# Rows of a 4-expert layer go back to their tokens by scatters inside the block loop instead of by gathers behind it

## What is computed

```python
x = x + 0.5 * _L0_ffn_ref(_layernorm(x), W1, b1, W2, b2, Wg, bg)   # 4 experts, one per token
x = x + _L0_attn_ref(_layernorm(x), ...)                          # "attention 0", no score matrix
x = x + 0.5 * _L0_ffn_ref(_layernorm(x), ...)                     # 4 experts again
x = x + 0.5 * _L1_ffn_ref(_layernorm(x), expert_sel, keys, values)  # 32 experts, top 4
x = x + _L1_attn_ref(_layernorm(x), ...)                          # softmax attention, 16 heads
x = x + 0.5 * _L1_ffn_ref(_layernorm(x), ...)                     # 32 experts again

# _L0_ffn_ref: the expert with the highest gate logit, alone, counts for a token
idx = argmax(softmax(x @ Wg + bg))
y[e] = gelu(x @ W1[e] + b1[e]) @ W2[e] + b2[e]
out = y[idx]
```

## Time and profile before

| | us |
|---|---|
| three runs | 2506.00, 2508.28, 2508.82; median 2508.28 |
| the profiled execution | 2506.18 |
| its span in the trace | 2504.4 |

### The profile page before, as it was taken

The page is one execution under the profiler, slowest core; times in us unless marked ns, Lnnn a source line. Parts: engine busy times, 40 slices in busy tenths (PEclk is TensorE's granted clock), DMA queues, the critical chain, the costliest instruction groups (busy, mean ns, idle before and its releaser), DMA issues.

```text
span 2504.4 us, 36012 instructions
## 1 busy us (share of the span) xinstructions
PE 2246.4 (90%) x11234; PEld 1562.8 (62%) x11234; DVE 1981.3 (79%) x4636; ACT 1297.6 (52%) x1907; POOL 991.8 (40%) x849
## 2 busy tenths in 40 slices
PE   4489488849869999996999999999999999999999
PEld 3367366637647777774555555555555555778777
DVE  5578487748759999976888888888888886888887
ACT  1088332338724444442666666666666665444444
POOL 5600688620056777752222111121111213565654
PEclk9999665569979999997999999999999999999999
DMA  7144221134268888861122211112111115888897
GB/s 177 61 161 139 38 32 37 30 113 153 93 139 177 182 178 177 184 140 54 57 68 69 63 59 60 59 56 61 59 56 60 57 55 108 175 178 183 176 185 153
DMA packets 148497, 266.81 MB, mean 107 GB/s; under 512 B 19347, under 2 KB 30614, under 8 KB 148118
## 3 DMA queue, kind: packets, MB, share of 16 engines
q1 hardware_dynamic: 132790, 247.99, 41.0%
q0 software_dynamic: 15584, 17.25, 3.3%
HBM read 213.26 MB, written 54.31 MB: 107 GB/s over the span
## 4 chain that ended last, share of the span: by engine, by line
PE 41%; DVE 5%; DMA 5%; issue 3%; ACT 1%; POOL 0%; SPq 0%; DVEq 0%; POOLq 0%; ACTq 0%
PE ps L2010 12%; PE ps L2034 10%; PE ps L2021 9%; DMA gate_rows<-gates_dram 4%; DVE m L1408 2%; PE ps L1729 2%; PE ps L1731 2%; PE ps L1730 2%; PE ps L2043 1%; PE ps L2076 1%; DMA gates_dram<-gateT 1%; DVE shift L1575 1%; DVE lo L1070 1%; PE ps L1743 1%; PE ps L2068 1%
## 5 line engine op out<-in xcount | busy, mean ns | idle before, releaser
L1575 DVE TENSOR_REDUCE shift<-ps 128x1 fp32r<-128x512 f32 x1024 | 663.6, 684 | 146.5 <-PE ps L2010 141.7
L993 ACT ACTIVATE prob<-ps 128x1024 f32<-128x1024 f32 x512 | 509.9, 1024 | 352.8 <-PE ps L2021 345.1
L842 ACT ACTIVATE hi<-m 128x512 fp32r<-128x512 f32 x512 | 318.9, 631 | 414.2 <-DVE m L1408 414.1
L692 POOL TENSOR_TENSOR lo<-m,hi 128x512 fp32r<-128x512 f32 x256 | 342.3, 1339 | 305.8 <-ACT hi L842 305.2
L2010 PE MATMUL ps<-k_pad,q_st 128*128 128x512 f32 x1024 | 401.0, 433 | 13.2 <-DVE shift L1575 7.0
L1408 DVE SCALAR_TENSOR_TENSOR m<-ps,gate_rows 128x512 f32<-128x512 f32 x512 | 334.4, 679 | 84.1 <-PE ps L1731 51.2
L2010 PEld LDWEIGHTS ps<-k_pad,q_st 128*128 128x128 f32 x1024 | 179.2, 190 | 256.0 <-DVE shift L1575 175.6
L2021 PE MATMUL ps<-q_sh,k_pad 128*128 128x512 f32 x1024 | 330.3, 404 | 0.0
L2034 PE MATMUL ps<-prob,v_cols 128*32 128x512 f32 x2048 | 272.8, 605 | 0.4 <-ACT prob L993 0.4
L1070 DVE TENSOR_TENSOR lo<-m,hi 128x512 fp32r<-128x512 f32 x256 | 210.5, 822 | 16.9
L1729 PE MATMUL ps<-hi,vals_hl 128*128 128x512 f32 x512 | 209.6, 409 | 0.7 <-DVE lo L1070 0.4
(11 more groups left out here) (218 smaller groups left out, 3996.5 us busy)
## 6 DMA issues: line engine op xcount, KB each, us to landing
gate_rows<-gates_dram SPq DMA_DIRECT2D x256, 512.0 KB, 6.3
w_blk<-w_dram SPq DMA_DIRECT2D x38, 514.5 KB, 3.6
q_st<-q_dram SPq DMA_DIRECT2D x64, 256.0 KB, 2.6
k_pad<-k_dram SPq DMA_DIRECT2D x256, 50.0 KB
k_dram<-qk_hl SPq DMA_DIRECT2D x48, 256.0 KB
q_dram<-qk_hl SPq DMA_DIRECT2D x48, 256.0 KB
x_blk<-sorted_x SPq DMA_DIRECT2D x38, 256.0 KB, 3.4
sorted_y<-yb_rows SPq DMA_DIRECT2D x38, 256.0 KB, 2.0
```

What stands on the lines that cost most here:

```text
L692: pool.tensor_tensor(m["lo"][:, s], m["m32"][:, s], m["hi"][:, s].bitcast(F32), ALU.subtract).then_inc(sig(ph, "lo_pool"), 1)
L842: return act.activation(o, i, ACT.Copy)
L993: act.activation(prob[:, h % HP, 2 * half:2 * half + 2, :], ps[:, b0:b0 + 2, :], ACT.Exp, scale=SCALE).then_inc(sig(ph, "prob"), 1)
L1575: dve.tensor_reduce(shift[:, g % 2, b, c:c + 1], wide(PASS1 + b % 2), AXX, ALU.max, negate=True).then_inc(sig(ph, "qmax"), 1)
```

## The change

- Each row of `sorted_x` is 129 floats wide (`DX`): the 129th is the number of its token. `apply_norm` copies it beside the normalised row, from a constant `token` that SP loads at the start. The filler rows behind an expert's last row carry the number `NOWHERE` = 16384, beyond every token; so do 512 rows at the end of `sorted_x`, where blocks without work now read (one more fill on SP in ph 0).
- SP's `save`, `plan_back`, `y_row`, `y_idx` and all gathers of output rows go. Instead Pool runs `scatter_y(ph)` during the layer, ahead of its barrier: per block one copy of the token numbers to int32 (`y_goes_to`, two blocks ahead) and four indirect DMAs that scatter `yb_rows` to the tokens' rows of `y_dram`; indices above 8191 are left out (`bounds_check`). `y_rows` of block n waits until these of block n-2 have landed.
- After ph 0 `collect(t)` is one plain accumulating DMA per tile on Pool, from 512 consecutive rows of `y_dram`. In ph 3 SP loads the rows plainly (`rows_back`): tiles 0 to 2 behind the barrier, every other tile behind the `gates` of the tile two before it; VectorE waits for `rows_here`.
- The plan of the blocks has one step more.

The core of the diff:

```diff
+DX = D + 1
+NOWHERE = 2 * TOKENS
...
+    c["token"] = (SEQ * np.arange(TILES)[None, :, None] + BLK * np.arange(P)[:, None, None]
+                  + np.arange(BLK)[None, None, :]).astype(np.float32).reshape(P, -1)
...
+            sp.dma_start(token[:], const["token"]).then_inc(early_in, 16)
...
-                    sp.dma_start(free, zeros[:]).then_inc(filled, 16)
+                    sp.dma_start(free, nobody[:]).then_inc(filled, 16)
+                if ph == 0:
+                    sp.dma_start(sorted_x[ROWS0:ROWS0 + SEQ, :].rearrange("(p s) d -> p s d", s=BLK),
+                                 nobody[:]).then_inc(filled, 16)
...
+                    if i >= WB:
+                        sp.wait_ge(sig(ph, "y_to"), n0 + i - WB + 1)
...
-                def save(i):
-                    n, q = n0 + i, (n0 + i) % 2
-                    sp.wait_ge(sig(ph, "yb_rows"), n + 1)
-                    sp.dma_start(sorted_y[i * SEQ:i * SEQ + SEQ, :].rearrange("(p s) d -> p s d", s=BLK),
-                                 yb_rows[q][:]).then_inc(y_there[q], 16)
...
-                        sp.wait_ge(filled, 16 * E0 * (turn + 1))
+                        sp.wait_ge(filled, 16 * (E0 * (turn + 1) + 1))
                     load_x(i)
-                for i in range(NB0):
-                    if i + WB < NB0:
-                        load_w(i + WB)
-                        load_x(i + WB)
-                    save(i)
+                for i in range(NB0 - WB):
+                    load_w(i + WB)
+                    load_x(i + WB)
...
+            def rows_back(n, q):
+
+                if not (isinstance(n, int) and n < 2):
+                    pass_wait(sp, sig(2, "x_done"), n * 4 - 4)
+                sp.dma_start(y_back[q][:], y_dram[bass.ds(n * SEQ, SEQ), :].rearrange("(p s) d -> p s d", s=BLK))\
+                  .then_inc(rows_here[q], 16)
+
+            sp.wait_ge(phase_end, 4 * 3)
+            for q in range(2):
+                sp.wait_ge(y_there[q], 64 * ((2 * NB0 + 1 - q) // 2))
+            for n in range(3):
+                rows_back(n, n % 2)
             gates(0, 0, first=True)
...
-            with sp.Fori(1, PAIRS) as pair:
-                gates(pair * 2, 0)
-                gates(pair * 2 + 1, 1)
+            rows_back(3, 1)
+            with sp.Fori(1, PAIRS - 1) as pair:
+                for q in range(2):
+                    gates(pair * 2 + q, q)
+                    rows_back(pair * 2 + (2 + q), q)
+            gates(TILES - 2, 0)
+            gates(TILES - 1, 1)
...
-                    if ph == 3 and gather and fb in (0, 2, 4, 6):
-                        collect_on(t, 1 - p, fb // 2)
...
-                def collect_on(t, q, b):
-
-                    if b == 0:
-                        pass_wait(pool, sig(ph, "y_idx"), t + 1)
-                    pool.indirect_dma_start(
-                        y_back[q][:, b, :], None, sorted_y,
-                        bass.IndirectOffsetOnAxis(ap=y_idx[:, q, b:b + 1], axis=0)).then_inc(back[q], 16)
...
-                        for n in range(3):
-                            collect(2, n)
...
+            def y_goes_to(ph, i):
+
+                n = FIRST_BLOCK[ph] + i
+                pool.wait_ge(w_here[n % WB], 32 * (n // WB + 1))
+                pool.tensor_copy(y_to[:, n % 4], x_blk[n % WB][:, :, D]).then_inc(sig(ph, "y_to"), 1)
+
+            def scatter_y(ph):
+
+                for i in range(2):
+                    y_goes_to(ph, i)
+                for i in range(NB0):
+                    n = FIRST_BLOCK[ph] + i
+                    pool.wait_ge(sig(ph, "yb_rows"), n + 1)
+                    if i + 2 < NB0:
+                        y_goes_to(ph, i + 2)
+                    pool.wait_ge(sig(ph, "y_to"), n + 1)
+                    for b in range(BLK):
+                        pool.indirect_dma_start(
+                            y_dram, bass.IndirectOffsetOnAxis(ap=y_to[:, n % 4, b:b + 1], axis=0),
+                            yb_rows[n % 2][:, b, :], None, bounds_check=TOKENS - 1,
+                            oob_is_err=False).then_inc(y_there[n % 2], 16)
...
+            def collect(t):
 
                 if t == 0:
-                    pool.wait_ge(sig(ph, "y_row"), ph // 2 + 1)
                     for q in range(2):
-                        done = ph // 2 * NB0 + NB0
-                        pool.wait_ge(y_there[q], 16 * ((done + 1 - q) // 2))
-                if t >= 2 and ph == 0:
-                    pool.wait_ge(sig(1, "stats"), t - 1)
-                elif t >= 2:
-                    pool.wait_ge(sig(ph, "x_done"), 4 * (t - 1))
-                for b in range(BLK):
-                    c = t * BLK + b
-                    rows = bass.IndirectOffsetOnAxis(ap=y_row[:, c:c + 1], axis=0)
-                    if ph == 0:
-                        pool.indirect_dma_start(x[:, c, :], None, sorted_y, rows,
-                                                compute_op=ALU.add).then_inc(back[t % 2], 16)
-                    else:
-                        pool.indirect_dma_start(y_back[t % 2][:, b, :], None, sorted_y,
-                                                rows).then_inc(back[t % 2], 16)
+                        pool.wait_ge(y_there[q], 64 * ((NB0 + 1 - q) // 2))
+                else:
+                    if t >= 2:
+                        pool.wait_ge(sig(1, "stats"), t - 1)
+                pool.dma_start(x[:, t * BLK:t * BLK + BLK, :],
+                               y_dram[t * SEQ:t * SEQ + SEQ, :].rearrange("(p s) d -> p s d", s=BLK),
+                               accum_op=ALU.add).then_inc(back[t % 2], 16)
...
                 scatter(0, t)
+            scatter_y(0)
             barrier(pool, 1)
...
             barrier(pool, 2)
+            scatter_y(2)
             barrier(pool, 3)
...
+                    dve.tensor_copy(dst[:, :, D], token[:, t * BLK:t * BLK + BLK])
...
-                dve.wait_ge(back[t % 2], 64 * (ph // 2 * (TILES // 2) + t // 2 + 1))
+                dve.wait_ge(rows_here[t % 2], 16 * (t // 2 + 1))
...
+                    pc.step(dve.tensor_scalar(begin_f[:], row_f[:], last_row[:, 0:1], float(2 * ROWS0), ALU.is_gt,
...
-                        dve.wait_ge(y_there[n % 2], 16 * (n // 2))
+                        dve.wait_ge(y_there[n % 2], 64 * (n // 2))
...
-                    if i == 1:
-                        plan_back()
...
-                    if ph == 3 and two_on and fb == 13:
-                        dve.tensor_copy(y_idx[:, p], y_row[:, bass.ds((t + 4) * BLK, BLK)])\
-                           .then_inc(sig(ph, "y_idx"), 1)
...
-                        dve.wait_ge(back[p], (t - p) * 32 + 64 * (TILES // 2 + 2))
+                        dve.wait_ge(rows_here[p], (t - p) * 8 + 32)
```

More of the change, by code:

```diff
@@ L47 @@
 NB0 = TILES + E0 - 1
+FIRST_BLOCK = {0: 0, 2: NB0}
 ROWS0 = REGION * E0
+DX = D + 1
+NOWHERE = 2 * TOKENS
 WCOL = 2 * FF0
@@ L209, in macaron @@
         with ExitStack() as first_own:
-            xnr_a = [first_own.enter_context(nc.sbuf_tensor(f"xnr_a{b}", [P, BLK, D], F32)) for b in range(XR)]
+            xnr_a = [first_own.enter_context(nc.sbuf_tensor(f"xnr_a{b}", [P, BLK, DX], F32)) for b in range(XR)]
             stage = [first_own.enter_context(nc.sbuf_tensor(f"stage{b}", [P, 2048], F32)) for b in range(2)]
@@ L225, in macaron @@
         w_hl = [ffn0_sb(f"w_hl{b}", [P, 2, WCOL], F32R) for b in range(2)]
-        x_blk = [ffn0_sb(f"x_blk{b}", [P, BLK, D]) for b in range(WB)]
+        x_blk = [ffn0_sb(f"x_blk{b}", [P, BLK, DX]) for b in range(WB)]
         xb_hl = xnT_hl
         ffn0_own.close()
-        sorted_x = nc.dram_tensor("sorted_x", (ROWS0, D), F32).ap()
-        sorted_y = nc.dram_tensor("sorted_y", (NB0 * SEQ, D), F32).ap()
+        sorted_x = nc.dram_tensor("sorted_x", (ROWS0 + SEQ, DX), F32).ap()
+        y_dram = nc.dram_tensor("y_dram", (TOKENS, D), F32).ap()
         w_dram = nc.dram_tensor("w_dram", (E0, P, WROW), F32).ap()
@@ L251, in macaron @@
         outT = att0_sb("outT", [P, SEQ])
-        xnr_b = [att0_sb(f"xnr_b{b}", [P, BLK, D]) for b in range(XR)]
+        xnr_b = [att0_sb(f"xnr_b{b}", [P, BLK, DX]) for b in range(XR)]
         xnr = {0: xnr_a, 2: xnr_b}
@@ L315, in macaron @@
         back = [sem(f"back{b}") for b in range(2)]
+        rows_here = [sem(f"rows_here{b}") for b in range(2)]
         w_here = [sem(f"w_here{b}") for b in range(WB)]
@@ L616, in _ @@
             pool.memset(neg_half[:], -0.5)
-            pool.memset(zeros[:], 0.0).then_inc(setup, 1)
+            pool.memset(nobody[:, :, 0:D], 0.0)
+            pool.memset(nobody[:, :, D:DX], float(NOWHERE)).then_inc(setup, 1)
             def rstd_of(ph):
@@ L686, in apply_norm, with step @@
                                        ALU.mult).then_inc(sig(ph, "xn"), 1)
-                def step(t, fb, two_on, p=0, gather=False):
+                def step(t, fb, two_on):
                     if fb in POOL_FB:
@@ L811, in _ @@
                     over_tiles(pool, ph, *low_parts(ph, ffn1_mem)[0:2])
```

(21 more changed lines are left out.)

37 lines of the change are left out of this document (15 added, 22 removed).

## The result

The changed kernel takes 2495.73 us (median of 6 runs, 2493.38 to 2499.78), the one before 2507.32 us (6 runs, 2503.92 to 2508.82): a ratio of 0.9953, 95% interval 0.9942 to 0.9963, so 11.6 us less, where 4.1 less were forecast. The profiled executions, one of each kernel, have spans of 2504.4 and 2491.5 us.

The account below looks back on a forecast made before the run. Pool was taken to bound attention 0, TensorE the 4-expert loop and 32-expert layer. Terms -12.8, +1.0, 0.0, +3.8, +2.9, +1.0 sum to -4.1 us: 2504.2 us from median 2508.28; range 2499 to 2509, whole 2494 to 2534.

Parts of the forecast that it names:

- Attention 0, -12.8: Attention 0: one plain accumulating load replaces four gathers on Pool, VectorE's waits go, token copy adds 1.4; -12.8 us.
- The third rival: Attention 0 and first boundary: the plain accumulating load costs Pool what four gathers did, 7.4 us; 2533 us; chance 0.09.
- The block loop, +1.0: 4-expert block loops: scatters bring Pool to 7.0 us a block, casts may wait a little; +1.0 us for both loops.
- The second rival: 4-expert block loop: Pool becomes the bound; 2531 us if a bounds check costs 0.2 us; chance 0.22.
- Both ends of the loop, 0 and +3.8: Boundaries behind the 4-expert layers: barriers left later, shorter loads pay back; 0.0 at the first, +3.8 us at the second.
- The drain: Barriers behind the 4-expert layers: a Pool drain behind indirect DMAs costs 5.0 us, as read behind attention 0.
- part 5: 32-expert layer: 60 gathers leave Pool and 15 index copies leave VectorE, booked at 0; late rows +1.0 us.
- the first rival: Ends of 4-expert loops: drain only waits for landing, or Pool needs 5.5 us a block; 2495 us; chance 0.18.
- Routing, +2.9: Routing of layer 0: fifth fill +1.4, token load +0.5, 16 small copies +1.0; together +2.9 us.
- The 32-expert layer, +1.0: 32-expert layer: y rows queued behind the gates delay each tile some 0.2 us; 13 tiles, +1.0 us in all.
- The fourth rival: 32-expert layer: rows land 2 us late in every tile, +0.9 us a tile; 2515 us; chance 0.06.

Follow-up runs that it names:

- number 8: Changed kernel with one fill of 128x1024 on Pool in each block of both 4-expert layers: 2505.0 us beside 2507.43 for the kernel before.
- number 9: Changed kernel with two fills of 128x1024 on Pool in each block of both 4-expert layers: 2520.71 us, ratio 1.0072 to the kernel before.
- number 3: Changed kernel; Pool waits for its scatters' semaphores instead of draining at the barriers behind both 4-expert layers and attention 0: 2486.25 us, ratio 0.9912.
- number 2: Kernel before, with one more Pool drain in an idle gap in the last tile of the first 32-expert layer: 2503.81 us beside 2508.38.
- number 10: Kernel before with only the wide rows: 129 floats, token copies, token load, fifth fill; ratio 1.0003.
- number 1: Changed kernel with one extra 64 KB Pool DMA at the start of the first 32-expert layer: ratio 0.9960 to the kernel before.
- number 4: Changed kernel; in the first 32-expert layer SP loads y rows ahead of the gates instead of behind them: 2493.19 us.
- number 11: The changed kernel run again, no edit: ratio 0.9948 to the kernel before.
- number 5: Changed kernel; three barriers without drain, y rows ahead of gates, remaining drain in a gap before attention 1: 2471.16 us beside 2502.78.
- number 6: Changed kernel with extra plain 2 KB Pool DMAs, 14 in the first 32-expert layer and four a tile in attention 1: 2490.93 us beside 2502.78.
- number 7: Changed kernel with extra indirect Pool gathers, 15 in the first 32-expert layer and 56 in attention 1: 2509.47 us beside 2502.78.

## Why the prediction was right or wrong

**Attention 0, -12.8: right, by parts that were each off by about 1 us.** Between `xn` of tile 0 and barrier 2 the changed kernel takes 224.9 us for 236.05: 11.2 less, with 1.6 us of a longer drain in it, which is -12.8. In parts: the ramp gave 2.0 for 2.8 (`xn` of tile 5 at 339.23 for 342.29, so from -1.0 to -3.1); from there to the last `xnr_b` (495.81 for 510.46) it is 11.6, where 11.4 of waits less 1.4 of copies were booked, that is 10.0; Pool's scatters behind it end 0.8 us later. The period is 12.12 us for the 12.07 of the earlier trace rows, so the token copy costs some 0.05 and not 0.1. The load takes 0.96 us of Pool for the 1.9 taken, which doesn't matter where Pool waits. The third rival (7.4 us a load) falls.

**The block loop, +1.0: right in sum, by two errors.** Pool was reckoned at 7.0 us a block and needs 5.9. The disturbance was the mis-sized term: 0.4 us a block instead of 1.6 (all 152 scatters have a mean of 1062 ns and a median of 979), the copy 0.19 us for 0.4. I had let every subtraction of VectorE stop a starting DMA. The loop costs nothing (108.9 us between the second and the next to last `yb_rows` in both kernels); the stretch from the first cast to the second `yb_rows`, in which `plan_back` stood, is 0.4 and 0.6 us shorter, which I had put at nothing; the last rows wait 1.0 us longer at each layer, which I had not seen. The second rival was near: numbers 8 and 9 put its point one fill of 0.95 us a block above the changed kernel, and show that it starts softly, over VectorE's casts. A bounds check of 0.2 us, +0.8 us a block, would have come close to it; but scatters with it take 0.97 us for the 0.95 without, so it costs next to nothing.

**Both ends of the loop, 0 and +3.8: off by -1.4 and -1.6, with larger errors inside that cancel.** Pool ends at 275.8 for 277.6 reckoned, but the drain takes 7.7 us for 5.0, so the barrier is left at 283.5, reckoned 282.6. `xn` of tile 0 stands at 292.15 for 293.1, since load 2 holds Pool 0.9 us ahead of the root, not 1.9. The first load starts at 284.43 and the statistics at 288.77, 4.3 us later and 3.35 after the end of Pool's work on the load (0.99 us); the load at 289.94 lets the statistics go at 293.99, 3.2 us after Pool's work on it. The prediction took 3.0 us for this. The formula of the Trainium skill (DMA: Bandwidth & Descriptors, Anatomy of one DMA) gives an estimate of 2.6 us for 256 KB on Pool's path; the trace is longer than both. At the second boundary it is +2.1 for +3.8: Pool's first `rstd` work began 17.6 us behind the end of VectorE's last rows (680.25 to 697.89) and now begins 19.7 behind it (668.32 to 688.01). SP's first load lands 2.8 us after its issue, for which I took 3.4.

**The drain: the step that failed.** I read 5.0 us at the earlier trace rows, took it for a fixed price behind indirect DMAs and added it where the change adds DMAs. I did not ask where the same price stood in the kernel before and would go: at barrier 4, ahead of which the change takes out 72 gathers, the 60 of part 5 and the 12 of the first three tiles. Part 5 says "60 gathers leave Pool ... 0", and this is the term that was missing, -5.2. Nor did barrier 2 stay at 5.0 (+1.6). Of the first rival one half was near, that Pool is hardly disturbed (5.9 us a block; it had 5.5). The other half had the drain as a wait for landing, 2 us: numbers 3 and 2 refute it. With the drain's price as measured, the barriers behind the loops cost 4.0 us more than the prediction booked (2.7 and 1.3), where this rival had them 6 us cheaper. That its 2495 us was met is luck.

**Routing, +2.9: probably too much.** Alone the wide rows cost 0.9 us (number 10), though 2.9 is within its interval. The pair of traces shows -0.2, but that is chance: in six other executions with wide rows (numbers 1, 3, 4, 8, 10, 11) the first cast of block 0 stands at 128.9 to 130.1, and in number 2, without them, at 127.70, so the stage costs some 1.2 to 2.4 us. (Numbers 5, 6, 7 and 9 ran on another chip, at 121.9 to 122.6; no trace without wide rows is there to compare.) One term was clearly too large: the four fills take 3.87 us for 5.43, and the fifth 0.44 instead of 1.4.

**The 32-expert layer, +1.0: too little.** The rows land 17.3 us behind their issue, as reckoned (17.1), VectorE waits 0.9 us a tile for them, and the chain over root and norm carries it on. The net price of a tile was right, 0.2 us (25.54 for 25.36), but of two terms where the prediction had one: late rows cost 0.4 (number 4), and the gathers and index copies that went, which part 5 has at 0, give back 0.2. What failed is the sum: 13 tiles of 0.2 are 2.6 us, and 1.0 was booked without a reason. The 3.2 us of the pair are these, 12 tiles of 0.19, and 0.9 in the first three tiles, which is noise as far as is known: from the first write of the gates to the fourth it took 76.7 us in the kernel before, but 79.5 in number 2 and 77.8 in number 10. The fourth rival (2 us late) falls.

In sum, against what was booked, for the traced pair: -3.1 in the routing, -1.4 and -1.6 at the two boundaries, +1.6 at barrier 2, +2.2 in ph 3, -5.2 at barrier 4, and -1.3 of small ones (as much lies between the last gates of ph 3 and Pool's arrival at barrier 4, where the granted clock was 0.96 for 0.93): the 8.8 us by which the pair gained more than 4.1.

## What to carry to other kernels

When a price is found for an operation ("a drain behind Pool's DMAs takes 5 us"), look for every place in the kernel before where it is already paid: a change that moves DMAs from one engine to another takes it away there as surely as it adds it here. Where a barrier stands behind Pool's DMAs, wait for their semaphores instead of draining, and put the one drain that is needed into a gap; that was worth more here than the change itself (some 15 of the 20 us of number 5; the rest is the rows' order). The place of a load in a queue behind 4 MB of other traffic is part of its time, and an engine that is not full can still lengthen another's instructions.

## What the runs showed of the hardware

- A drain of Pool costs about 0.08 us for each DMA that Pool has issued since its last drain, up to 7.7 us, hundreds of microseconds after they have landed (7.71 us, number 3), and a second drain behind the first adds nothing that shows (0.76 us, ended by VectorE, number 2). With 64 gathers that add among 128 it was 5.0 us; this is open.
- A plain accumulating load of 256 KB costs Pool 0.87 to 0.96 us where nothing disturbs it and lets its reader go 4.05 to 4.3 us after its start; an accumulating gather of 64 KB costs Pool 1.54 us.
- A load of 256 KB on SP lands 2.8 us after its issue with nothing ahead of it in the queue, and 17.3 us after it behind 4 MB in the same queue (ph 3 of the changed kernel).
- Beside Pool's scatters VectorE's fp32 casts of 128x512 have a mean of 493 ns for 419 without them, and of 556 ns with a fill of 128x1024 a block more (number 8; all three from 160 to 250 us).
